# Attention scores from three one-pass products of high and low parts, in place of one exact four-pass product

## The reference

```
keys    = einsum('bse,neh->bsnh', x, W_key)   + Bias_key
queries = einsum('bse,neh->bsnh', x, W_query) + Bias_query
scores  = einsum('bknh,bqnh->bnqk', keys, queries) / 8
scores  = where(q < k, 1e-10, scores)            # masked keys keep a weight
probs   = softmax(scores);  weighted = einsum(probs, values);  out = einsum(weighted, W_output)
```

## Time and profile before

| | |
|---|---|
| median of three runs | 2325.91 us |
| profiled execution | 2326.83 us |
| its span, first to last instruction | 2325.0 us |
| TensorE matmul busy | 2240.2 us, 96% |
| VectorE busy | 1230.7 us, 53% |
| ScalarE busy | 899.9 us, 39% |
| GpSimd busy | 1345.7 us, 58% |
| first score product of pair 0 starts | 90.47 us |
| mean granted TensorE clock | 0.984 |

### The profile page before, as it was taken

How to read it: one execution, slowest core, us unless ns; L and a number is a source line. 1 busy time by engine, 2 the same in 40 slices (tenths; PEclk the granted TensorE clock), 3 DMA queues, 4 the chain that set the end, 5 groups by cost and what they waited for, 6 DMA issues and landing times. The chain is left out here.

```text
span 2325.0 us, 33962 instructions
## 1 busy us (share of the span) xinstructions
PE 2240.2 (96%) x11872; PEld 1032.7 (44%) x11872; DVE 1230.7 (53%) x3455; ACT 899.9 (39%) x1764; POOL 1345.7 (58%) x1212
## 2 busy tenths in 40 slices
PE   6999999999999999999999999999999998899987
PEld 2334343434343434343434343434343435777764
DVE  5655555545454556454646464636363662466654
ACT  2244444444444446444444444444444441110110
POOL 1277777777777767676767676767676711111110
PEclk9799999999999999999999999999999998999998
DMA  1001010101010111010110111010102013411100
GB/s 49 12 13 48 18 47 17 48 17 48 17 48 17 48 53 39 26 39 26 31 35 30 35 31 34 30 35 30 35 30 64 30 42 118 164 64 46 64 19 18
DMA packets 117192, 93.71 MB, mean 40 GB/s; under 512 B 67552, under 2 KB 84128, under 8 KB 117024
## 3 DMA queue, kind: packets, MB, share of 16 engines
q1 hardware_dynamic: 117024, 91.55, 12.7%
HBM read 69.21 MB, written 21.76 MB: 39 GB/s over the span
## 5 line engine op out<-in xcount | busy, mean ns | idle before, releaser
L672 POOL TENSOR_TENSOR acc<-acc,probs 128x512 f32<-128x512 f32 (+1 forms) x900 | 984.0, 1126 | 328.5 <-ACT probs L1014 327.6
L1014 ACT ACTIVATE probs<-ps_s 128x512 f32<-128x512 f32 (+1 forms) x1152 | 582.6, 573 | 617.1 <-PE ps_s L819 393.4
L1071 DVE TENSOR_REDUCE partial<-ps_bg 128x1 f32<-128x512 f32 x768 | 487.5, 683 | 300.8 <-PE ps_bg L759 300.6
L817 PE MATMUL ps_s<-q_all,k_all 64*128 64x512 f32 (+3 forms) x2560 | 604.5, 543 | 0.0
L841 PE MATMUL ps_o<-probs,v 128*64 128x512 f32 (+3 forms) x2560 | 538.2, 541 | 0.0
L819 PE MATMUL ps_s<-max_rows,max_gate 64*128 64x512 f32 (+3 forms) x1280 | 454.2, 695 | 0.0
L707 PE MATMUL ps_bg<-home,w_in 128*128 128x512 f32 x768 | 382.0, 620 | 12.8 <-ACT q_bf L924 7.1
L1068 DVE CUSTOM_DVE_ANT_0 junk<-ps_bg,mask_q 128x512 bf16<-128x512 f32 (+3 forms) x512 | 230.2, 484 | 177.1 <-issue 175.9
L759 PE MATMUL ps_bg<-k_bf,q_bf 64*128 64x512 bf16 (+3 forms) x1280 | 273.6, 361 | 11.6 <-DVE den_rows L1102 3.2
L817 PEld LDWEIGHTS ps_s<-q_all,k_all 64*128 64x128 f32 x2560 | 228.6, 189 | 73.9 <-issue 54.0
L841 PEld LDWEIGHTS ps_o<-probs,v 128*64 128x64 f32 x2560 | 155.3, 136 | 236.0 <-issue 196.0
(11 more groups left out here) (114 smaller groups left out, 1778.4 us busy)
## 6 DMA issues: line engine op xcount, KB each, us to landing
e<-masked_weights SPq DMA_DIRECT2D x128, 128.0 KB, 2.9
scale<-inverse_sums SPq DMA_DIRECT2D x128, 128.0 KB, 2.9
heads_turned<-num SPq DMA_DIRECT2D x64, 256.0 KB, 2.0
c_o_in<-heads_turned SPq DMA_DIRECT2D x6, 2048.0 KB, 7.6
home<-in_L_attn_residual SPq DMA_DIRECT2D x8, 512.0 KB, 4.9
c_o_in<-heads_turned SPq DMA_DIRECT2D x8, 512.0 KB, 10.0
c_x_in<-in_L_attn_residual SPq DMA_DIRECT2D x8, 512.0 KB, 8.4
out<-c_y SPq DMA_DIRECT2D x8, 512.0 KB, 2.9
```

The source lines that it names most:

```text
L672: g.tensor_tensor(acc[h][:, group % 2, q0:q0 + w], acc[h][:, group % 2, q0:q0 + w], probs[h][:, probs_slot(i, t), at:at + w], ALU.add).the ...
L817: pe.matmul(out[h], k_all[HEAD[h], i % 2, kb * P:(kb + 1) * P], q_all[HEAD[h], i % 2, q], start=True, stop=False, skip_group_check=True)
L1014: nc.scalar.activation(probs[h][:, probs_slot(i, t), CH * half:end], ps_s[:, k % SCORE_BANKS, 0:end - CH * half], ACT.Exp, scale=SCORE_SCA ...
L1071: e.reduce_max(to, of, AX.X).then_inc(max_read, 1)
```

## The change

The exact tiles `q_all` and `k_all` go. In their place stand `q_hi`, `q_lo`, `k_hi`, `k_lo` in fp32r, for two pairs each. ScalarE writes the high part where it wrote the exact value, VectorE then reads the same PSUM bank once more, adds the bias, subtracts the high part and writes the low part. The score product becomes three fp32r products: high by high, high keys by low queries, low keys by high queries, each for both heads, with the waits of both heads ahead of the first. The bank of every projection is now given free by VectorE (`proj_read`). To make room, the feed-forward weights are staged in `vt`, `q_bf` and `k_bf`, and are loaded one pair later, once these tiles are dead.

```
-    counts = {"proj_qk": 0, "proj_v": 0, "max": 0, ...}
+    counts = {"proj": 0, "max": 0, ...}
...
-        staged = [sb(f"staged{b}", [P, 4, CH]) for b in range(2)]
...
-        q_all = sb("q_all", [P, 2, S])
-        k_all = sb("k_all", [P, 2, S])
+        q_hi = sb("q_hi", [P, 2, S], F32R)
+        q_lo = sb("q_lo", [P, 2, S], F32R)
+        k_hi = sb("k_hi", [P, 2, S], F32R)
+        k_lo = sb("k_lo", [P, 2, S], F32R)
...
+        staged = [vt[:, :].rearrange("p (l t) -> p l t", l=4),
+                  q_bf[:, :].bitcast(F32).rearrange("p (l t) -> p l t", l=2)]
+        lora_in = k_bf[:, :].bitcast(F32).rearrange("p (l t) -> p l t", l=2)
...
                 def load_weights(j):
-                    sp.wait_ge(bf_ready, START + 8 * j)
-                    sp.wait_ge(v_read, START + 4 * j)
+                    sp.wait_ge(proj_read, START + NPROJ * j)
...
                 def load_ffn_weights():
-                    sp.wait_ge(proj_done, START + NPROJ * N)
+                    sp.wait_ge(proj_read, START + NPROJ * N)
+                    sp.wait_ge(max_read, START + 2 * NMAX * N)
+                    sp.wait_ge(sums_ready, START + 4 * N)
+                    sp.wait_ge(fin_written, START + fin_before(N - 1, fin_index("vt", 0)) + 1)
...
-                    if i + 2 == N:
+                    if i + 1 == N:
                         load_ffn_weights()
...
                     if t == 0:
-                        pe.wait_ge(hi_ready, START + 8 * (i + 1))
+                        pe.wait_ge(proj_read, START + NPROJ * (i + 1))
...
                         out.append(ps_s[:, k % SCORE_BANKS, at % CH:at % CH + w])
-                        pe.matmul(out[h], k_all[HEAD[h], i % 2, kb * P:(kb + 1) * P], q_all[HEAD[h], i % 2, q],
-                                  start=True, stop=False, skip_group_check=True)
+                    keys = slice(kb * P, (kb + 1) * P)
+                    for h in range(2):
+                        pe.matmul(out[h], k_hi[HEAD[h], i % 2, keys], q_hi[HEAD[h], i % 2, q], start=True, stop=False,
+                                  skip_group_check=True)
+                    for h in range(2):
+                        pe.matmul(out[h], k_hi[HEAD[h], i % 2, keys], q_lo[HEAD[h], i % 2, q], start=False, stop=False,
+                                  skip_group_check=True)
+                    for h in range(2):
+                        pe.matmul(out[h], k_lo[HEAD[h], i % 2, keys], q_hi[HEAD[h], i % 2, q], start=False, stop=False,
+                                  skip_group_check=True)
...
                 def low(j, u):
                     c, m = PROJ_CHUNKS[u // 3], u % 3
-                    if m < 2:
+                    if m == 2:
+                        dve.wait_ge(proj_done, START + NPROJ * j + u + 1)
+                        e.tensor_scalar(vt[:, cols(c)], bank("proj", j, u), bias[:, 2:3], None,
+                                        ALU.add).then_inc(proj_read, 1)
                         return
-                    dve.wait_ge(proj_done, START + NPROJ * j + u + 1)
-                    e.tensor_scalar(vt[:, cols(c)], bank("proj", j, u), bias[:, 2:3], None,
-                                    ALU.add).then_inc(v_read, 1)
+                    dve.wait_ge(hi_ready, START + 8 * j + 2 * (u // 3) + m + 1)
+                    dve.wait_ge(bf_ready, START + 8 * j + 2 * (u // 3) + m + 1)
+                    high_part, low_part = ((q_hi, q_lo), (k_hi, k_lo))[m]
+                    e.scalar_tensor_tensor(low_part[:, j % 2, cols(c)], bank("proj", j, u), bias[:, m:m + 1],
+                                           high_part[:, j % 2, cols(c)].bitcast(F32), ALU.add, ALU.subtract
+                                           ).then_inc(proj_read, 1)
```

More of the change, by code:

```diff
@@ L177, in background @@
     first, users = {}, []
-    counts = {"proj_qk": 0, "proj_v": 0, "max": 0, "fin": 0, "den": 0, "ln": len(PROJ_CHUNKS), "lora": 0, "weight": 0}
+    counts = {"proj": 0, "max": 0, "fin": 0, "den": 0, "ln": len(PROJ_CHUNKS), "lora": 0, "weight": 0}
     for use in order:
         kind = {"vt": "fin", "mt": "fin"}.get(use[0], use[0])
-        if kind == "proj":
-            kind = "proj_v" if use[2] % 3 == 2 else "proj_qk"
         first[use] = len(users)
@@ L272, in attention @@
         la_in = [xs[0:R, 3, l // 2, (l % 2) * D:(l % 2 + 1) * D] for l in range(4)]
-        la_in += [staged[1][0:R, 2, l * D:(l + 1) * D] for l in range(2)]
-        lbt = [staged[1][0:R, 3, l * D:(l + 1) * D] for l in range(2)]
+        la_in += [lora_in[0:R, 0, l * D:(l + 1) * D] for l in range(2)]
+        lbt = [lora_in[0:R, 1, l * D:(l + 1) * D] for l in range(2)]
         lb_in = w_in[:, 0].rearrange("p m h -> p (m h)").rearrange("p (l e) -> p l e", e=R)
@@ L310, in attention @@
         hi_ready = sem("hi_ready")
-        v_read = sem("v_read")
+        proj_read = sem("proj_read")
         bf_ready = sem("bf_ready")
@@ L406, in load_ffn_weights @@
                                  lora_a[0:4].rearrange("l r d -> r l d")).then_inc(ffn_w_loaded, 16)
-                    sp.dma_start(staged[1][0:R, 2].rearrange("r (l d) -> r l d", d=D),
+                    sp.dma_start(lora_in[0:R, 0].rearrange("r (l d) -> r l d", d=D),
                                  lora_a[4:n_layers].rearrange("l r d -> r l d")).then_inc(ffn_w_loaded, 16)
@@ L695, in bank_read @@
                         reader, count = users[k - BANKS]
-                        pe.wait_ge({"proj_qk": bf_ready, "proj_v": v_read, "max": max_read, "fin": fin_read, "den": den_read, "ln": xs_ready,
+                        pe.wait_ge({"proj": proj_read, "max": max_read, "fin": fin_read, "den": den_read, "ln": xs_ready,
                                     "lora": lora_ready, "weight": wt_ready}[reader], START + count)
@@ L919, in high @@
                     act.wait_ge(proj_done, START + NPROJ * j + u + 1)
-                    exact = (q_all, k_all)[m]
-                    nc.scalar.activation(exact[:, j % 2, cols(c)], bank("proj", j, u), ACT.Identity,
+                    high_part = (q_hi, k_hi)[m]
+                    nc.scalar.activation(high_part[:, j % 2, cols(c)], bank("proj", j, u), ACT.Identity,
                                          bias=bias[:, m:m + 1]).then_inc(hi_ready, 1)
```

## The result

The changed kernel takes 2316.41 us, the median of eight runs (2305.23 to 2318.6), against 2326.41 of the kernel before (eight runs, 2324.53 to 2327.19). The ratio is 0.9942, 95% interval 0.9928 to 0.9955. Forecast were 2280. So the kernel became faster by 10 us where 46 were expected; the number lies in the range of 2256 to 2322. The changed kernel's profiled execution was its shortest run, 2305.23 us (span 2303.4); that of before had 2326.83. Between the two executions that were traced, the gain is 21.6 us.

A forecast was written before the change was run, and what follows sets the result against it. The prediction took TensorE to set the pace of all sixteen pairs, VectorE having little room beside the maxima. Its terms, -105 + 33 + 20 + 6 = -46 us, took 2326.83 to 2281, median 2280, range 2256 to 2322.

The forecast's parts named there:

- rival B: Behind the projections VectorE becomes the bound, nearly no gain beside the maxima: loss 65 us, 2325 us; chance 0.22.
- score passes: Score products: four fp32 passes become three fp32r passes, -105 us together, 6.6 per pair.
- the bound named in the prediction: Score products: if each one-pass product costs the gate's 0.23 us, a full block is 0.92; bound -85 us.
- VectorE beside the maxima: Beside the maxima, three places per pair where TensorE waits for VectorE's reads lose 1.3 us: +20 us.
- low parts in 15 pairs: Projections: VectorE's extra read holds the bank longer, 2.11 us instead of 1.32; 2.2 us per pair, +33 us.
- ahead of the loop: Projections of pair 0: six hand-overs longer by 0.79 us, plus VectorE's statistics behind the low parts; +6 us (0 to 9).
- I take 0.215: Score products: price in us of an added fp32r pass inside a full block, giving a block of 0.875.
- blocks 0.92 or more apart: Sign of being wrong: starts of full score blocks this far apart in us, where 0.87 to 0.88 was expected.
- rival D: Score products: weight loads show, each pass costs 0.213 + 0.11 us, a full block 1.29; 2475 us, chance 0.03.
- Rival C: Projections: all eight q and k reads put their whole 0.79 us on TensorE's path, 6.3 per pair; 2342 us, chance 0.13.
- A: Rival: the whole gain arrives, VectorE's reads come in time, only +12 us or so lost; 2235 us, chance 0.10.
- a clock below 2.4 GHz within the pairs: Sign of being wrong: a lower granted clock in the pairs, since longer gaps would then cost twice; no size given.

The follow-up runs named there:

- x1: Changed kernel with the low parts not computed but set to zero once, banks freed by ScalarE's second read; 2266.74 us, 0.9745 of the kernel before.
- x4: Changed kernel with high and low parts in bf16 in place of fp32r; 2277.61 us, 0.9785 of the kernel before.
- x3: Changed kernel with ScalarE reading the bank once and making the bf16 rounding from the high part in SBUF; 2272.79 us, 0.9759 of the kernel before.
- x9: Changed kernel with nine unused products ahead of the first turned feed-forward weight; 2312.08 us, five runs, 0.9935 of the kernel before.
- x12: Changed kernel with three unused products (512, 512 and 256 wide) ahead of the first turned feed-forward weight; 2305.0 us, four runs, 0.9909 of the kernel before.
- x7: Changed kernel measured again, unchanged; 2307.57 us, four runs, 0.9917 of the kernel before.
- x8: Kernel before with only the feed-forward weights staged in the dead tiles and loaded one pair later; 2326.96 us, eleven runs, 0.9997 of the kernel before.
- x2: Changed kernel with the four-pass fp32 product put back on the high parts, low parts computed but unused; 2371.11 us, 1.0187 of the kernel before.
- x11: Changed kernel measured a third time, unchanged; 2309.71 us, six runs, 0.993 of the kernel before.
- x6: Changed kernel with bf16 parts and the rounding made from the high part, no filler; 2234.84 us, five runs, 0.9618 of the kernel before.

## Why the prediction was wrong

The mechanism was right and the sign with it. Wrong is above all a size, and one term was missing. The range held the result partly by its width: 2316.41 lies outside the forecast's own range (2262 to 2302) and inside the band of rival B (2302 to 2326), whose mechanism did not occur. Both columns are for traced executions until the last row; x1 separates the low parts from the products. The first two rows are not measured one by one: the first is the spacing of the starts times the count, the second what is then left.

| term | forecast | found | from |
|---|---|---|---|
| score passes | -105 | -85 | 0.23 a pass, the bound named in the prediction |
| VectorE beside the maxima | +20 | +18 | x1 against before is -67; -67 + 85 |
| low parts in 15 pairs | +33 | +37 | 1735.4 - 1698.1 |
| ahead of the loop | +6 | +9 | 99.2 - 90.2 |
| behind the pairs | 0 | -1 | |
| sum, traced | -46 | -22 | |
| lower clock in most runs, median over the traced run | none | +11 | 2316.41 - 2305.23 |

*Score products: the step that failed.* "I take 0.215: the step from fp32 to the gate, between separate products of one bank, cost nothing extra." That step ended an fp32 record; what follows the gate itself, 0.23 in the earlier trace rows, was the only fp32r row at hand, and I read its extra as belonging to the change of block. Every fp32r pass pays it. The operation that was to be added stood in the trace, with its price; I priced it by its neighbours. That is 20 of the 24 us that the traced executions miss. The prediction's own sign of being wrong, "blocks 0.92 or more apart", is what the trace shows.

*The weight loads.* The Trainium skill's rule ("TensorE: Matmul & The Clock Gate", Part 3) stood beside rival D: with equal row groups loads wouldn't overlap, and 2475 us was the sum. The trace disagrees: passes of the same rows with a 0.19 us load each are 0.23 apart, which leaves no room for it. The Trainium skill, on the same page, Part 2, section "Back-to-back issue gap", gives N / 2.4 + 2.5 ns as the isolated gap of one product, 216 ns for 512 columns, and about 131 ns for sustained streams of loads and products. x4's stream agrees with the first figure: its bf16 passes are 0.2155 us apart, each with two heads' products side by side. For fp32r the trace has 0.23, and the measurement decides.

*The low parts* cost 2.4 us per pair against 2.2 forecast, for the reason given: a hand-over of 2.17 us, and x3 takes it away with VectorE's work unchanged. Rival C wanted 5.3 per pair and isn't borne out, nor is A.

*VectorE beside the maxima* bounds at places such as tile 9, with about 1.1 us lost per pair (18 / 16) for 1.3 forecast. The loss is a difference, but it lies where it was looked for: from before to x1, tiles 0 to 7 became 2.3 us shorter, where their passes at 0.23 save 2.4, and tiles 8 to 19, beside the maxima, 1.9 where they save 3.0. Rival B, nothing gained there at all, fell: from before to after, on average tile 8 became 0.34 us shorter (two blocks at 0.17), tile 12 0.29, tile 14 0.22, tile 10 0.20 and tile 9 nothing.

*Ahead of the loop* 9 and not 6. I summed six waits of 0.79 and a little. From one projection to the next, five steps grew by 0.86 and one by 1.27, 5.6 in all; the granted clock fell behind one wait, and the projection of 3.61 us adds 1.6; 1.1 more came behind the last projection, where that of 58.50 took 2.87 us instead of 1.98, at a fallen clock again. The start of pair 0 lay between 98.2 and 101.3 in the traces of the changed kernel and its filled versions.

*The missing term.* In the first measurement five of eight runs lay about 11 us above the other three, at mean granted clocks of 0.975 to 0.977 against 0.982. I had written of a clock below 2.4 GHz within the pairs only; there it stayed at 2.4. One place where it falls is behind TensorE's wait ahead of the turned weights, 1.7 to 2.6 us in the kernels with one-pass products; the other is ahead of the loop, as above. In the trace of before it waits 1.09 us there, and one group behind takes 2.08 as well, but the 42 runs of that kernel in the comparisons lie between 2324.2 and 2332.5. x9 and x12 show that with this wait filled the runs lie close together, at 2304 to 2308 in x12, and x4's trace that nearly the whole passage at 1.2 GHz costs 11 to 12 us. Two things stay open. None of the runs near 2318 was itself traced, so that most of their 11 us lie here is inferred; x7's trace has 2 us in either place. And why the wait grew isn't settled: not through the staging alone (x8 has 1.1), but x1, without low parts, has 2.4 and x2, without the three products, 2.0.

## What to carry to other kernels

Price an added operation by the row of its own kind and type, even if it is only one row in a mixed block, before the neighbours' rows. A new read of a PSUM bank is priced by the length of the chain of readers until the bank is free, and not by the busy time of the engine that reads: let one reader copy out and make the other forms from the copy, so that two engines work at once. And where runs of one kernel spread, look for idle stretches of TensorE and for the granted clock behind them; with 2.2 us of junk products there the median was 2305.0, against 2307.6, 2309.7 and 2316.4 without.

## What the hardware showed that I had not expected

- An fp32r pass costs more than one in bf16 or half of an fp32 record: 0.23, 0.2155 and 0.215 us at 512 columns; at 128 columns 0.112 against 0.056 in bf16.
- The granted clock fell to 1.2 GHz behind waits of TensorE of 1.1 to 2.6 us, and not behind each of them: the projection of 45.59 took 3.61 us, the one behind the next equal wait (54.30, idle for 1.88) 1.98. In the changed kernel's own trace the weights behind 1.89 us ran at full clock, in x11's behind 2.13 they didn't.
- How long the clock then stays down varies too, 3.4 us in the trace of x6 (behind a wait of 2.25), 37 in that of x4 (behind 2.57), though TensorE had no gap in the turned weights in either.
